# A quarter of the row-picking masks of two graph attention passes: made by ScalarE in an earlier pass and loaded, instead of made by GpSimd in place

## The reference

```python
# first layer: weighted sum of neighbours
neighbor = segment_sum(w[:, None] * x[src], dst)
out = leaky_relu(x @ W1.T + b1 + (neighbor + neighbor * x) @ W2.T + b2)
x = layernorm(x + out / max(norm(out), eps))
# second and third: transformer convolution, 4 heads of 64
def tconv(x, Wq, Wk, Wv, We, Ws, ...):
    e = edge_attr @ We                       # 194 attributes an edge
    kj, vj = k[src] + e, v[src] + e          # k, q, v: projections of x
    logits = einsum('ehc,ehc->eh', q[dst], kj) / sqrt(64)
    a = softmax of logits over the edges of one dst
    return segment_sum(vj * a, dst) + x @ Ws + bs
h = relu(tconv(x, ...1)); x = layernorm(x + tconv(h, ...2))
```

## Time and profile before

| | us |
|---|---|
| median of 3 runs | 4497.03 (4490.62 to 4498.63) |
| profiled execution, its own time | 4498.7 |
| its span, first to last instruction | 4496.9 |
| PE busy | 4109.7 (91%) |
| VectorE busy | 3759.8 (84%) |
| GpSimd busy | 3210.1 (71%) |
| ScalarE busy | 3036.2 (68%) |
| granted PE clock, mean | 0.987 |

### The profile page before, as it was taken

The page is one execution under the profiler, slowest core; times in us unless marked ns, Lnnn a source line. Parts: engine busy times, 40 slices in busy tenths (PEclk is TensorE's granted clock), DMA queues, the critical chain, the costliest instruction groups (busy, mean ns, idle before and its releaser), DMA issues. The chain is left out here.

```text
span 4496.9 us, 108726 instructions
## 1 busy us (share of the span) xinstructions
PE 4109.7 (91%) x17720; PEld 3175.0 (71%) x17720; DVE 3759.8 (84%) x20610; ACT 3036.2 (68%) x10782; POOL 3210.1 (71%) x3078
## 2 busy tenths in 40 slices
PE   5999999998979999999999998979999999999996
PEld 4887877775657777777777775557777777777764
DVE  5655555556979999999999998889999999999996
ACT  2333333333518988889898895139999999999983
POOL 6777777773067888778787782188888888888842
PEclk9999999999999999999999999999999999999999
DMA  5887887774678888888888884588888888888855
GB/s 171 255 250 236 247 242 241 237 234 134 204 235 257 260 257 256 255 253 258 259 261 250 253 265 122 181 253 259 259 255 255 257 258 255 256 259 256 260 156 160
DMA packets 770941, 1064.81 MB, mean 237 GB/s; under 512 B 111323, under 2 KB 588728, under 8 KB 770277
## 3 DMA queue, kind: packets, MB, share of 16 engines
q0 software_dynamic: 171184, 540.40, 40.1%
q1 hardware_dynamic: 599094, 517.47, 38.1%
HBM read 906.27 MB, written 151.16 MB: 235 GB/s over the span
## 5 line engine op out<-in xcount | busy, mean ns | idle before, releaser
L1476 POOL DMA_INDIRECT e_kv<-kv,src x1664 | 1662.6, 999 | 536.7 <-issue 301.1
L1709 ACT ACTIVATE e_vals<-e_kvj,e_ex 128x65 f32<-128x65 f32 x6572 | 1686.7, 334 | 0.1
L1497 PE MATMUL e_q<-q,e_pick 128*128 x3328 | 1056.2, 399 | 144.7 <-DVE e_logit L1604 113.7
L1604 DVE CUSTOM_DVE_ANT_0 e_kvj<-e_kvj,e_q 128x64 f32<-128x64 f32 x6656 | 1062.7, 215 | 4.3 <-PE e_q L1497 0.4
L153 POOL DMA_INDIRECT rows_x<-x_rows,rows_src x783 | 745.2, 952 | 243.5 <-issue 174.3
L1497 PEld LDWEIGHTS e_q<-q,e_pick 128*128 128x128 f32 x3328 | 576.6, 190 | 434.7 <-issue 369.4
L1539 PE MATMUL e_sum<-e_vals,e_mask 128*128 128x260 f32 x2536 | 784.8, 391 | 20.4 <-ACT e_vals L1709 9.4
L1592 DVE TENSOR_TENSOR e_kvj<-e_kv,e_e 128x512 f32<-128x512 f32 x1110 | 752.8, 678 | 54.9 <-DMA e_kv<-kv,src 28.6
L1487 PE MATMUL e_e<-e_we,e_ea 112*128 112x256 f32 x2220 | 670.6, 383 | 39.4 <-DMA e_ea<-attr_tiles 39.3
L1468 POOL TENSOR_SCALAR e_pick<-e_spots,own 128x512 f32<-128x512 bf16 x416 | 688.5, 1655 | 17.8 <-DMA e_spots<-locals 4.3
L1665 DVE TENSOR_TENSOR acc<-acc,e_sum 128x260 f32 x1602 | 668.5, 417 | 33.9 <-PE e_sum L1539 22.8
(11 more groups left out here) (226 smaller groups left out, 4904.3 us busy)
## 6 DMA issues: line engine op xcount, KB each, us to landing
e_ea<-attr_tiles SPq DMA_DIRECT2D x1110, 112.0 KB
edges<-q SPq DMA_DIRECT2D x277, 256.0 KB
e_made<-edges SPq DMA_DIRECT2D x554, 128.0 KB
e_spots<-locals SPq DMA_DIRECT2D x416, 128.0 KB
q<-attr_tiles SPq DMA_DIRECT2D x277, 112.0 KB
e_kv<-kv,src POOLq DMA_INDIRECT x1664
e_plain<-masks SPq DMA_DIRECT2D x396, 64.0 KB
masks<-q SPq DMA_DIRECT2D x208, 64.0 KB
```

What stands on the lines that cost most here:

```text
L1476: e.indirect_dma_start(out=kv[:, u, :], out_offset=None, **rows_of(kv_rows, k["src"][:, i:i + 1])).then_inc(kv_got[u], 16)
L1497: e.matmul(pe_q[i % 2][:, 0:D], pick[:, c, at:at + P], rows, start=True, stop=True).then_inc(q_done, 1)
L1604: dot = e.tensor_tensor_reduce(kvj[:, i % 2, h, 0:C], kvj[:, i % 2, h, 0:C], pe_q[i % 2][:, hs], 1.0, 0.0, ALU.mult, ALU.add, logit[:, j % ...
L1709: by_weight = e.activation(vals[:, n % R, h * HV:(h + 1) * HV], kvj[:, 2 + n % NV, h, :], ACT.Copy, scale=ex[:, b % 2, h, r:r + 1])
```

## The change

In the first edge pass ScalarE also makes the turned mask of the first step of each quad, with the same two activations. SP loads that step's 128 positions to all partitions (bf16) for it, and stores the mask to a new table `picks`. In the attention passes SP loads this mask into the first quarter of `pick`, GpSimd makes the other three quarters in one instruction of 384 columns, and the load of the positions is cut to three rows. The query of a quad's first step waits for the load, those of the other three for GpSimd.

```diff
+class TurnedMasks:
...
+    def load(self, e, c):
+        if c >= 2:
+            e.wait_ge(self.apart_done, c - 1)
+        e.dma_start(self.spots[:, c % 2, :], self.locals16[c * QUAD:c * QUAD + 1, :].to_broadcast([P, P])
+                    ).then_inc(self.spots_got[c % 2], 16)
+
+    def make(self, e, c):
+        e.wait_ge(self.spots_got[c % 2], 16 * (c // 2 + 1))
+        if c:
+            e.wait_ge(self.made, c)
+        e.activation(self.apart, self.spots[:, c % 2, :], ACT.Square, bias=self.k["own"][:, 0:1], scale=-1.0).then_inc(self.apart_done, 1)
+        e.wait_ge(self.apart_done, c + 1)
+        if c >= 2:
+            e.wait_ge(self.stored[c % 2], 16 * (c // 2))
+        e.activation(self.masks[c % 2], self.apart, ACT.Relu, bias=self.k["one"][:, 0:1], scale=-1.0).then_inc(self.made, 1)
+
+    def store(self, e, c):
+        e.wait_ge(self.made, c + 1)
+        e.dma_start(self.table[c * P:(c + 1) * P, :], self.masks[c % 2]).then_inc(self.stored[c % 2], 16)
...
@@ edge_pass_weighted, SP @@
+            turned.load(e, 0)
             for i in range(T):
...
                 if i % QUAD == 2:
                     plain.store(e, i // QUAD)
+                if i % QUAD == 3 and i // QUAD + 1 < s.quads:
+                    turned.load(e, i // QUAD + 1)
+                if i % QUAD == 0 and i:
+                    turned.store(e, i // QUAD - 1)
...
             edges.store(e, s.trios - 1)
+            turned.store(e, s.quads - 1)
             own.all_stored(e)
             first.begin(e)
             edges.all_stored(e)
             plain.all_stored(e)
+            turned.all_stored(e)
@@ edge_pass_weighted, ScalarE @@
                 if i % QUAD == 1:
                     plain.make(e, i // QUAD)
+                if i % QUAD == 3:
+                    turned.make(e, i // QUAD)
@@ edge_pass_attention, SP @@
-                    e.dma_start(spots[:, c % 2, :], locals16[c * QUAD:(c + 1) * QUAD, :].rearrange("s c -> (s c)").unsqueeze(0)
-                                .to_broadcast([P, QUAD * P])).then_inc(spots_got[c % 2], 16)
+                    e.dma_start(spots[:, c % 2, :], locals16[c * QUAD + 1:(c + 1) * QUAD, :].rearrange("s c -> (s c)").unsqueeze(0)
+                                .to_broadcast([P, (QUAD - 1) * P])).then_inc(spots_got[c % 2], 16)
+
+                def load_pick(c):
+                    if c >= 2:
+                        e.wait_ge(q_done, (c - 2) * QUAD + 1)
+                    e.dma_start(pick[:, c % 2, 0:P], picks_made[c * P:(c + 1) * P, :]).then_inc(pick_got[c % 2], 16)
...
                 e.dma_start(we[:], w_edge).then_inc(w_got, 16)
                 load_spots(0)
+                load_pick(0)
...
                     if i % QUAD == 0 and i // QUAD + 2 < T // QUAD:
                         load_spots(i // QUAD + 2)
+                    if i % QUAD == 1 and i // QUAD + 1 < T // QUAD:
+                        load_pick(i // QUAD + 1)
@@ edge_pass_attention, GpSimd @@
-                    e.tensor_scalar(pick[:, c % 2, :], spots[:, c % 2, :], k["own"][:, 0:1], None, ALU.is_equal).then_inc(picked, 1)
+                    e.tensor_scalar(pick[:, c % 2, P:], spots[:, c % 2, :], k["own"][:, 0:1], None, ALU.is_equal).then_inc(picked, 1)
@@ edge_pass_attention, PE @@
-                    e.wait_ge(picked, i // QUAD + 1)
+                    if i % QUAD:
+                        e.wait_ge(picked, i // QUAD + 1)
+                    else:
+                        e.wait_ge(pick_got[i // QUAD % 2], 16 * (i // QUAD // 2 + 1))
```

More of the change, by code:

```diff
@@ L591, in all_stored, with __init__, edge_pass_weighted @@
             e.wait_ge(self.stored[u], 16 * ((self.s.quads - u + 1) // 2))
-def edge_pass_weighted(nc, ph, k, t, s, ring, begun, own_table, edge_table, mask_table, first):
+class TurnedMasks:
+    def __init__(self, ph, k, s, locals16, table, room):
+        self.k, self.s, self.locals16, self.table = k, s, locals16, table
+        self.apart, self.masks = room[:, 0:P], [room[:, (1 + u) * P:(2 + u) * P] for u in range(2)]
+        self.spots = room[:, 3 * P:4 * P].bitcast(BF16).rearrange("p (u c) -> p u c", u=2)
+        self.spots_got, self.stored = ph.sems("turned_spots_got", 2), ph.sems("turned_stored", 2)
+        self.apart_done, self.made = ph.sem("turned_apart"), ph.sem("turned_made")
+    def load(self, e, c):
[15 more added lines that the diff above has]
+        e.dma_start(self.table[c * P:(c + 1) * P, :], self.masks[c % 2]).then_inc(self.stored[c % 2], 16)
+    def all_stored(self, e):
+        for u in range(2):
+            e.wait_ge(self.stored[u], 16 * ((self.s.quads - u + 1) // 2))
+def edge_pass_weighted(nc, ph, k, t, s, ring, begun, own_table, edge_table, mask_table, locals16, pick_table,
+                       first):
     T, R, SUMS = s.steps, 6, 4
@@ L607, in edge_pass_weighted @@
     plain = PlainMasks(ph, k, s, mask_table, k["q"][:, edges.width:])
+    turned = TurnedMasks(ph, k, s, locals16, pick_table, k["q"][:, edges.width + 3 * P:])
     sums = [ph.psum(f"sum{u}") for u in range(SUMS)]
@@ L1270, in _, with edge_pass_attention @@
                         tools.root(e, b)
-def edge_pass_attention(nc, name, k, t, s, w_edge, edge_rows_made, masks_made, kv_rows, pens, locals16, singles, skip_of, last):
+def edge_pass_attention(nc, name, k, t, s, w_edge, edge_rows_made, masks_made, picks_made, kv_rows, pens, locals16, singles, skip_of, last):
     PACE = 2
@@ L1297, in edge_pass_attention @@
         apart = ph.sb("apart", [P, P])
-        spots = ph.sb("spots", [P, 2, QUAD * P], BF16)
+        spots = ph.sb("spots", [P, 2, (QUAD - 1) * P], BF16)
         pick = ph.sb("pick", [P, 2, QUAD * P])
@@ L1328, in edge_pass_attention @@
             ph.sems("kv_got", NG), ph.sems("ea_got", NE), ph.sems("runs_got", 2), ph.sems("spots_got", 2))
-        made_got, plain_got = ph.sems("made_got", 2), ph.sems("plain_got", 2)
+        made_got, plain_got, pick_got = ph.sems("made_got", 2), ph.sems("plain_got", 2), ph.sems("pick_got", 2)
         w_got, cleared = ph.sem("w_got"), ph.sem("cleared")
@@ L1760, in build @@
     cols = [scratch(f"cols{c}", [P, KD, s.rows]) for c in (1, 2)]
-    edges, masks = scratch("edges", [s.trios * P, 2 * D]), scratch("masks", [s.quads * P, P])
+    edges = scratch("edges", [s.trios * P, 2 * D])
+    masks, picks = (scratch(name, [s.quads * P, P]) for name in ("masks", "picks"))
     skip = scratch("skip", [s.rows, D])
@@ L1772, in build @@
                 begun = make_tables(nc, k, t, s, pens, locals16, singles, ring)
-                edge_pass_weighted(nc, ph, k, t, s, ring, begun, own, edges, masks, first)
+                edge_pass_weighted(nc, ph, k, t, s, ring, begun, own, edges, masks, locals16, picks, first)
             node_pass_resnorm(nc, k, s, first, x1, kv[0], cols[0])
-        edge_pass_attention(nc, "e1", k, t, s, t["w_edge1"], edges[:, 0:D], masks, kv[0], pens, locals16, singles,
+        edge_pass_attention(nc, "e1", k, t, s, t["w_edge1"], edges[:, 0:D], masks, picks, kv[0], pens, locals16, singles,
                             (cols[0], w_skip1, b_skip1, skip), None)
@@ L1779, in build @@
             last = LastRows(outer, k, cols[1], x1, w_skip2, b_skip2)
-            edge_pass_attention(nc, "e2", k, t, s, t["w_edge2"], edges[:, D:2 * D], masks, kv[1], pens, locals16, singles,
+            edge_pass_attention(nc, "e2", k, t, s, t["w_edge2"], edges[:, D:2 * D], masks, picks, kv[1], pens, locals16, singles,
                                 None, last)
```

## The result

The changed kernel is slower: 4581.3 us in the median of its runs (4577.8 to 4584.3), against 4495.0 us for the kernel before (4490.6 to 4498.6). The ratio is 1.019, with an interval of 1.018 to 1.020. The forecast was 4482 us, and its range ended at 4503 us.

A forecast was written before the change was run, and what follows sets the result against it. It took GpSimd to bound the first edge pass and attention openings, VectorE to be fullest in the attention passes. From 4498.7 us, -7.5 - 12 - 1 + 0.8 + 2 + 1 = -16.7 us gave 4482 us, range 4460 to 4503.

The forecast's parts named there:

- some 2 us: End of the first edge pass: landings of the node pass's first loads, said to be covered by 7 us or more.
- (a) to (c): Attention passes, GpSimd's saving: both openings 7.5 us, rest of second pass 12 us, rest of first 1 us; together 20.5 us.
- Late attributes and traffic: Attention passes: new issue ahead of late attributes in the first costs 2 us; added DMA traffic costs 1 us.
- the heads of the passes: Start of both attention passes: the new load stands in front of the first attributes, costing 0.8 us in all.
- Cost 0: First edge pass: ScalarE's idle time covers the new activations, attributes are asked for two products ahead; upper end 1 us.
- GpSimd does not see any of it: First edge pass: GpSimd, which sets the pace, is untouched by the added ScalarE and SP work.
- The end of that pass: First edge pass's tail ends at 1029 to 1040 us instead of 1021, still covered; cost 0, or 6 us without cover.
- the 1048 us: Node pass: first loads issued after this time were named as a sign that the forecast is wrong.
- The rivals: VectorE stays the bound 0.30; DMA throughput 0.12; GpSimd bounds the second attention pass 0.08; first edge pass's tail, within forecast's 0.50.
- DMA throughput: Steady part of both attention passes: 257 GB/s is a ceiling, giving 4544 us; chance 0.12 with its partial form.
- Its partial form: Attention passes: a third of the DMA throughput slowdown, about 4505 us; included in that rival's 0.12.

The follow-up runs named there:

- a4: Changed kernel with the loaded quarter in a buffer of its own, three deep, and asked for one quad earlier: 4481.6 us, ratio 0.9971.
- b1: Changed kernel with the loaded quarter in its own two-deep buffer and SP storing the skip rows three steps later: 4486.1 us, ratio 0.9974.
- b2: Kernel before with one edit, SP storing the skip rows three steps later: 4476.9 us, ratio 0.996.
- c1: Changed kernel, but nothing made in the first edge pass and the fourth mask loaded once at the head of each attention pass: 4470.0 us, ratio 0.995.
- c2: Kernel before with one more load of 64 KB a quad in the attention passes, into a buffer nobody reads: 4501.4 us, ratio 1.0013.
- a3: Changed kernel with the first attention pass as before, so only the second loads the quarter: 4491.6 us, ratio 0.9996.
- c0: The changed kernel again with no edit, measured beside others on one chip: 4579.6 us, ratio 1.017.
- b4: Changed kernel with the quarter loaded a quad earlier, first edge pass order relaxed by deeper buffers, and skip store three steps later: 4443.6 us, ratio 0.988.

## Why the prediction was wrong

**The step that failed** is this one: "Its wait is for the query of five steps earlier, which PE has long done, so nothing is held up behind it: the mask is wanted three steps later in the loop, and SP keeps with GpSimd's picks, which are up to six steps ahead of VectorE." The first half nearly held: SP stood 12.6 and 12.0 us in all at that wait in the two passes. The second half took a distance in the program for a distance in time. GpSimd had made the quarter from positions loaded two quads ahead; the new load was asked for one quad ahead, on a queue that goes in step with PE. PE wanted the mask 5.8 us after its issue in the mean, and 2.3 to 4.3 us after it where SP had just stood at a skip store, against landings of up to 7.4 us. The sum priced the load as an issue (0.42 us) and as traffic (1 us), never as a landing; the only landing that the forecast names is "some 2 us", for another place. a4 changes only the lead, and the attention passes take 85 us less. b1 changes only the store that shortens the lead, and the first attention pass takes 94 us less, of which b2 puts 13 to 24 us to the store alone. That the lead is what costs is shown. How much of the loss is the waits themselves and how much the lower clock behind them is not.

The row that would have told it was at hand: SP's waits in the kernel before, 323 us for PE's edge product. The forecast read SP's timeline at the seams and not its waits.

**The openings and the stalls, (a) to (c)**: right in kind. The time from the first add to the first sum, 73.9 and 72.7 us before, is 70.0 and 71.0 us in c1, 3.9 and 1.7 us less (3.7 forecast). VectorE's wait for gathered rows in the second pass falls from 28.5 us to 8.1 us in the changed kernel, 6.6 of it in the opening, and to 11.7 us in c1. GpSimd's wait for VectorE rose to 98.6 us after the opening where over 100 was named. The second pass was sized too low, 15.7 us forecast and 19.2 measured. For the rest of the first pass (1 us forecast) c1 gives some 9 us against one profile of before, but profiles of the old order alone differ by 11 us, so its size stays open.

**Late attributes and traffic**: 4 us were forecast with the heads of the passes, 6 us measured in c2 with twice the net bytes, and not in the pass where the late attributes are. b2 shows the other side, which the forecast had as a row and not as a lever: without the stalls that it counted as 20.9 us the pass is 13 to 24 us shorter.

**First edge pass, "Cost 0"**: wrong in its reasons, and in size in part. It said that ScalarE's 595 us of idle time take in the new activations and that attributes are asked for two products ahead. Both were read from 120 us on, where the pass already runs at GpSimd's pace, and by engine and not by queue. The cover was not idle ScalarE but the order in SP's queue. "GpSimd does not see any of it" failed too: its gathers waited up to 3.1 us for sums that PE did late. Making the table alone costs 5 us by the medians, which can't be told from nothing (ratio 1.0006). In six profiles the pass ends 4.6 to 21 us late. How long GpSimd's gathers are held tells the two worst from the others; what makes the lag larger in one execution than in another is open, as is whether the time not lost there comes back as waits in the next pass. The granted clock doesn't order them: over 60 to 1040 us it is 0.984 in after, 0.993 in b1 and 0.991 in a3 and c0, against 0.990 before.

**The end of that pass**: the tail took longer than said, 17 turned-mask stores from 1022.1 to 1065.7 us, 2.7 us a quad where 1.7 to 2.5 were given, and the first load of the node pass was issued at 1066.2 us, past the 1048 us that was named as the sign. By the trace it decided nothing: the last late mask of GpSimd starts at 1066.0 us too, and the load that marks the node pass's beginning comes 8.5 us after the last sum, before and after alike.

**The rivals.** None of the four named the mechanism. The one on the slower side, DMA throughput, gave a time (4544 us) nearer to the measured one than the forecast's, by a reason that the runs refute. That shows how little a matching time says of a cause. Its partial form was also added up wrongly: a third of 53 us less 7.5 us gives 4509 us, not 4505. With the order of issue put right (a4), the kernel takes 4481.6 us where 4482 was said. Part of that is luck: the second pass gains 18.5 us (15.7 forecast), the first edge pass loses 7.4 us (0 forecast), and misses of opposite sign cancel.

## What to carry to other kernels

When work is replaced by a load, price the load by its landing: from when its queue will really issue it, which is read from that queue's waits, to when it is wanted, and compare this with the slowest landing under load. A distance in steps is no distance in time when the queue is in order, waits for the consumer's own buffers, and has a long wait of another kind in it. An extra buffer and one quad more of lead showed no cost here and were worth about 85 us in the attention passes.

Cover for added work in one stage must be looked for in the queue that feeds it and in its catch-up phase, not only in the idle time of the engine that does the work. And an engine that sets the pace sees a consumer's lateness as soon as its ring of buffers is used up.

One profile of each kernel doesn't size a gain of 10 us in one pass: look at the other kernels that run the same code there.

## What the runs showed of the hardware

- A load of 64 KB by SP's queue had landed 3.0 to 7.4 us after its issue (mean 5.2 over the 51 queries that waited, a choice toward late ones) with the DMA engines 0.85 busy. The Trainium skill (DMA: Bandwidth & Descriptors, "Anatomy of one DMA — SWDGE (gpsimd) path") fits a transfer's time as 2.0 us plus bytes over 436 GB/s, which is an estimate of 2.15 us for 64 KB. The page gives it for GpSimd's path. This case's trace doesn't agree for SP's queue beside busy DMA engines, and there the measurement decides.
- The DMA engines moved up to 269 GB/s over 1200 us at a share of 0.90.
- A comparison with 384 columns on GpSimd takes 1.265 us and one with 512 columns 1.585 us. Worked out from the two this is an estimate of 2.5 ns a column and 0.3 us beside it, so a quarter of the columns took off 20% of the time.
- TensorE's granted clock was 0.98 from 1400 to 2600 us after, and 1.00 before and in b4. At the end of each of the eight waits of 3 us or more for the mask, to 1.1 us, it fell to 0.50 for 3.4 or 6.8 us. At 2017 us a pair of matmuls then took 1.06 us instead of 0.59.
